# An attention block with a routed feed-forward: LayerNorm of transposed tokens along the partitions instead of transposing normalised tokens on TensorE

## What is computed

```python
x = x + xattn(layernorm(x), ctx)        # 16 heads of 64; ctx has 192 features
x = x + ffn(layernorm(x))               # 8 experts, the best 2 of each token

def layernorm(x): return (x - mean(x)) / sqrt(var(x) + 1e-5)      # over the 256 features
def xattn(x, ctx):
    q, k, v = x @ w_q, ctx @ w_k, ctx @ w_v                       # 256x1024, 192x1024
    return softmax(q k^T / 8) v @ w_o + b_o
def ffn(x):
    g = softmax(x @ gate); keep the 2 largest of 8, divide by their sum
    return sum over experts of g_e * (relu(x @ W1_e + b1_e) @ W2_e + b2_e)
```

## Time and profile before

| | |
|---|---|
| median of 3 runs | 1580.46 us (1580.43 to 1581.63) |
| the profiled execution | 1580.22 us |
| its span in the trace | 1578.5 us |
| PE busy | 1553.8 us, 98% |
| DVE, ACT, POOL busy | 75%, 70%, 52% |
| granted TensorE clock | 0.994 of full speed |

### The profile page before, as it was taken

One profiled execution on the slowest core, in us unless ns is written; L12 is line 12 of the kernel. 1 busy time (PEld: TensorE's weight loads), 2 busy tenths in 40 slices (PEclk: granted clock), 3 DMA queues, 4 the chain that ended last, 5 costly groups with the idle time before them and its releaser, 6 DMA issues.

```text
span 1578.5 us, 45424 instructions
## 1 busy us (share of the span) xinstructions
PE 1553.8 (98%) x14150; PEld 1454.0 (92%) x14151; DVE 1176.1 (75%) x3796; ACT 1108.0 (70%) x3357; POOL 818.1 (52%) x946
## 2 busy tenths in 40 slices
PE   8999999999999999999999999999999999999997
PEld 7899999999899999999999989998899999999997
DVE  4777777777777777777777777777788777777775
ACT  5677677677776777767767777676666676777774
POOL 2344545545554554554555455455456555555556
PEclk9999999999999999999999999999999999999999
DMA  6522111222111221211122211122799755555554
GB/s 201 145 72 74 60 60 60 77 90 72 62 60 60 67 94 66 74 60 60 63 75 89 74 60 60 60 67 81 241 231 249 144 86 85 89 86 90 84 84 61
DMA packets 105643, 145.05 MB, mean 92 GB/s; under 512 B 12736, under 2 KB 87616, under 8 KB 105344
## 3 DMA queue, kind: packets, MB, share of 16 engines
q1 hardware_dynamic: 60144, 89.00, 17.8%
q0 software_dynamic: 26816, 37.32, 13.7%
q10 hardware_dynamic: 18640, 18.19, 4.4%
HBM read 77.09 MB, written 67.38 MB: 92 GB/s over the span
## 4 chain that ended last, share of the span: by engine, by line
issue 47%; POOL 22%; PE 9%; DVE 7%; DMA 6%; DVEq 3%; ACT 2%; POOLq 2%; ACTq 1%; SPq 0%
POOL lists L662 7%; DMA out<-stage_room,number 6%; PE bank_a L1404 4%; POOL prob L669 3%; DVE hid L1332 3%; POOL rstd L648 2%; DVE stage_room L1349 2%; POOL stage_room L711 2%; POOL stage_room L707 2%; POOL out L735 2%; DVEq L1344 1%; PE bank_v L1437 1%; POOLq L729 1%; PE bank_s L1422 1%; DVEq L1323 1%
## 5 line engine op out<-in xcount | busy, mean ns | idle before, releaser
L669 POOL TENSOR_TENSOR prob<-prob,inv 128x512 f32<-128x512 f32 x256 | 271.4, 1060 | 520.3 <-DVE inv L956 519.6
L777 ACT ACTIVATE prob<-bank_s,low 128x128 f32<-128x128 f32 x1024 | 363.3, 376 | 40.9 <-DVE low L951 40.9
L735 POOL DMA_INDIRECT out<-stage_room,number x142 | 231.8, 1632 | 53.9 <-issue 53.1
L951 DVE TENSOR_REDUCE low<-bank_s 128x4 f32<-128x512 f32 x256 | 175.4, 685 | 98.0 <-PE bank_s L1422 97.9
L777 ACT ACTIVATION_READ_ACCUMULATOR prob<-bank_s,low 128x1 f32 x1024 | 221.1, 216 | 0.0
L770 ACT ACTIVATE probt<-bank_t 128x512 f32<-128x512 f32 x256 | 153.4, 599 | 89.6 <-PE bank_t L1411 89.6
L1050 DVE SCALAR_TENSOR_TENSOR stage_room<-xin,wo_t 128x256 f32<-128x256 f32 x480 | 178.8, 426 | 0.0
L807 ACT ACTIVATE ot_h<-bank_v 128x512 fp32r<-128x512 f32 x128 | 77.4, 604 | 138.4 <-PE bank_v L1437 138.4
L885 ACT ACTIVATE hidt_h<-hid 128x512 fp32r<-128x512 f32 x142 | 89.7, 632 | 117.4 <-DVE hid L1332 112.2
L1411 PE MATMUL bank_t<-ident,prob 128*128 128x128 f32 x1024 | 161.9, 281 | 4.0 <-POOL prob L669 4.0
L1404 PE MATMUL bank_a<-xt_l,wq_h 128*128 128x256 f32 x512 | 152.4, 298 | 0.3 <-DVE xt_l L966 0.3
(11 more groups left out here) (231 smaller groups left out, 4728.9 us busy)
## 6 DMA issues: line engine op xcount, KB each, us to landing
stage_room<-lists ACTq DMA_DIRECT2D x67, 265.0 KB
halves<-stage_room SPq DMA_DIRECT2D x32, 512.0 KB
homes<-halves SPq DMA_DIRECT2D x16, 1024.0 KB, 6.4
xin<-in_x SPq DMA_DIRECT2D x32, 256.0 KB, 2.8
stage_room<-in_x SPq DMA_DIRECT2D x32, 256.0 KB
stage_room<-in_w SPq DMA_DIRECT2D x32, 256.0 KB, 4.3
out<-stage_room SPq DMA_DIRECT2D x32, 256.0 KB, 2.2
cin<-in_ctx SPq DMA_DIRECT2D x32, 128.0 KB, 2.6
```

The costliest lines, as they stand in the source:

```text
L669: pool.tensor_tensor(prob[:, n % 4, :, :], prob[:, n % 4, :, :], wide(inv[:, n % 4, :], P), ALU.mult).then_inc(s_norm.sem, 1)
L735: pool.indirect_dma_start(out, bass.IndirectOffsetOnAxis(ap=number[:, u, b:b + 1], axis=0), ysum[:, u, b, :], None, compute_op=ALU.add).th ...
L777: e = act.activation(prob[:, n % 4, h, :], bank_s[n % 2][:, h * P:(h + 1) * P], ACT.Exp, bias=low[:, n % 4, h:h + 1], scale=-1.0, accum_ou ...
L951: dve.tensor_reduce(low[:, n % 4, :], bank_s[n % 2][:, :].rearrange("p (h k) -> p h k", h=4), AX.X, ALU.min).then_inc(s_low.sem, 1)
```

## The change

The host also passes `x_t`, the tokens transposed. SP loads the pair's 256 columns of it as `xraw` (feature per partition, between `xin` and `cin`). The statistics are still taken from `xin` by DVE and POOL, which now writes 1/sqrt over the variance in `mean_var`. SP (`ln_through`) waits for it, stores the 128x4 numbers to DRAM (`ln_rows`), waits for the store and loads them back as one row broadcast to all partitions (`ln_all`). DVE subtracts the mean and multiplies in place, two operations over 128x512 elements that read `ln_all` with a step of four words (`normalise_turned`, in slot 3 after the reciprocal). ACT writes the high part from `xraw` in slot 4, behind `copy_t` and ahead of `exps`; DVE writes the low part in slot 4 (`low_of_tokens`). Event `t0` with its four transposes is gone, and so are L1019's two operations into `xn`. The 15 remaining events get fixed banks (`BANK_OF`). The reciprocal of unit 3 moves from slot 4, behind `lowest`, to the end of slot 3. The three router scores of slot 3 are made in slots 1 and 2: 8, 6, 0 and 2. In pass -1 the broadcast is made by four matmuls instead of by DMA (`first_statistics`).

```diff
+    BANK_OF = {"q10": 0, "k10": 1, "o0": 2, "k11": 3, "q11": 0, "o1": 1, "v10": 2, "v11": 3,
+               "q00": 0, "k00": 1, "q01": 2, "k01": 3, "v00": 1, "f0": 0, "v01": 2}
-        [("o1", FROM0), ("t0", NEXT)],
+        [("o1", FROM0)],
...
+            def ln_through(sp, it):
+                if not isinstance(it, int) or it > 0:
+                    sp.wait_ge(ln_in, it * 16)
+                wait(sp, pool_step, it, "rstd1")
+                sp.dma_start(ln_rows, mean_var[:, 0, :, :]).then_inc(ln_out, 16)
+                sp.wait_ge(ln_out, it * 16 + 16)
+                wait(sp, xn_step, it - 1, "xn")
+                sp.dma_start(ln_all.rearrange("p t b k -> p (t b k)"), ln_rows.rearrange("t b k -> (t b k)").rearrange(
+                    "(o n) -> o n", o=1).to_broadcast([P, 4 * P])).then_inc(ln_in, 16)
...
                         load_x(it)
+                        ln_through(sp, it)
...
+                        if n == 4 and has(it, NEXT):
+                            wait(act, a_full, it, "q11")
+                            wait(act, xn_step, it, "xn")
+                            act.activation(xt[0][:, 0:DC, :], xraw.rearrange("p c b t -> p c (b t)"),
+                                           ACT.Copy).then_inc(xa_hi.sem, 1)
...
+                    dve.tensor_tensor(xraw[:, :, :, :], xraw[:, :, :, :], of_tokens(it, 0), ALU.subtract).then_inc(xn_step.sem, 1)
+                    wait(dve, xn_step, it, "centred")
+                    dve.tensor_tensor(xraw[:, :, :, :], xraw[:, :, :, :], of_tokens(it, 1), ALU.mult).then_inc(xn_step.sem, 1)
...
-                X_SCORES = {1: (0, 5), 2: (5, 6), 3: (11, 3), 5: (14, 2)}
+                X_SCORES = {1: [(0, 8)], 2: [(8, 3), (11, 3)], 5: [(14, 2)]}
...
-                    if kind == "t":
-                        wait(pe, ln1_step, it, "ln1")
-                        for b in range(2):
-                            for c in range(DC):
-                                last = pe.transpose(dst[:, (2 * c + b) * P:(2 * c + b + 1) * P],
-                                                    xn[:, b, c * P:(c + 1) * P], ident[:, :])
```

More of the change, by code:

```diff
@@ L359, in by_products, with a_bank @@
                 return isinstance(it, int) and it < 1
[L361 to L367, removed]
+            def a_bank(name):
+                return bank_a[BANK_OF[name]]
             def bank_before(it, name):
+                same = [n for n, _ in A_EVENTS if BANK_OF[n] == BANK_OF[name]]
                 if not isinstance(it, int):
[L372 to L376, removed]
+                    k = same.index(name) - 1
+                    return (it if k >= 0 else it - 1), same[k]
+                order = [(j, n) for j in range(-1, PAIRS + 1) for n in a_full.present(j) if n in same]
+                k = order.index((it, name)) - 1
                 return order[k] if k >= 0 else (it, None)
@@ L1035, in rows_of @@
                     dve.wait_ge(sent, (it - 1) * 64 + 16)
-                    normalise(it, 1, x1, [rows[:, b, 0:D] for b in range(2)])
+                    normalise(it, x1, [rows[:, b, 0:D] for b in range(2)])
                 def x_scores(it, first, many):
@@ L1140, in body @@
                         if n == 5 and has(it, NEXT) and not by_products(it):
-                            x_scores(it, *X_SCORES[n])
+                            for first, many in X_SCORES[n]:
+                                x_scores(it, first, many)
+                        if n == 4 and has(it, NEXT):
+                            low_of_tokens(it)
                         made_in = it - 1 if n == 0 else it
@@ L1184, in body @@
                             gate_max(it)
+                            after_step(it, "bn2_1")
+                        if n == 3 and has(it, NEAR[4][1]):
+                            inverse(it, NEAR[4][0], 3)
                         if n in X_SCORES and n < 5 and has(it, NEXT) and not by_products(it):
[L1186 removed]
+                            for first, many in X_SCORES[n]:
+                                x_scores(it, first, many)
                 steps_of_table = [0]
@@ L1567, in keep_busy, with first_statistics @@
                                   skip_group_check=True)
+                def first_statistics():
+                    wait(pe, pool_step, -1, "rstd1")
+                    pe.wait_ge(made, 20)
+                    for k in range(2):
+                        for b in range(2):
+                            last = pe.matmul(bank_s[1][:, (2 * k + b) * P:(2 * k + b + 1) * P],
+                                             mean_var[:, 0, b, k:k + 1].to_broadcast([P, P]), ident[:, :],
+                                             start=True, stop=True, skip_group_check=True)
+                    last.then_inc(ln_first, 1)
                 def gate_means():
```

118 lines of the change are left out of this document (68 added, 50 removed).

## The result

| | us, median (runs) | ratio to before, 95% interval |
|---|---|---|
| before | 1580.6 (6) | |
| changed | 1588.37 (1584.91 to 1589.22, 6 runs) | 1.0049 [1.0037, 1.0061] |

The changed kernel is slower by 0.5%, 7.8 us. That is above the 0.2% that can be told from nothing and outside the range of the forecast. The profiled execution took 1587.79 us with a span of 1586.0, 7.5 more than the span of before.

What follows compares the result with a forecast made beforehand. PE was taken as the bound, without gaps worth naming in the loop. 1580.22 us profiled + 0.7 start - 13.6 transposes + 13.3 chain gave 1580.6 us, no change, with a range of 1575 to 1586 us.

Steps and rivals of the forecast that it cites:

- The transposes, -0.44 us a pass.: PE between `o1` and `values`, slot 3: four transposes gone, 0.65 us becomes 0.21, at most 13.6 us in 31 passes.
- The chain of slot 4, +0.43 us.: From T, start of slot 4's PE transposes: ACT's copy delays DVE's low parts, `k00` loads 0.43 us late; 13.3 us.
- The early reciprocal: 0.: POOL scales unit 3 about 1.5 us earlier, clear of the tokens' low part; PE did not wait for that unit.
- may be lost here for nothing: DVE in slot 3: 1.7 us could be lost at no cost before the low part starts at T+1.85.
- the low part meets POOL's work and the chain grows by 0.1 to 0.2 us, 3 to 6 us: Rival, slot 4: slower by 3 to 6 us; 8% together with an overrun of slot 3.
- DVE in slots 1 to 3: 0.: Moved scores and two operations on `xraw` fit into freed waits and gaps: 0, at most 2 us in all.
- my bound of 1.46: Slot 3, DVE: longest time in us for each operation on `xraw`, where the 1.7 us are used up.
- my 0.61: Slot 3, DVE: lower time in us for each strided operation on `xraw`, what L1157 costs; 0.61 to 1.0 taken.
- The broadcast: 0.: Statistics through DRAM, slots 1 to 3: 6.0 us needed of 7.9 us, 1.9 us in hand.
- The start, +0.7.: Pass -1: 256 KB of `xraw` ahead of the weights PE waits for, +0.7 us, bounds 0 to 1.3.
- `k00` never waits: Extreme of the shorter-chain rival, slot 4: no wait, 1567.3 us; that rival had 20% for a gain over 3.2 us.

Runs made afterwards that it cites:

- b2: Kernel before, with three of the four transposes of the tokens left out in the looped passes: 1569.45 us, ratio 0.9932.
- d2: Changed kernel, unit 3's reciprocal right behind DVE's multiplication, POOL's last send behind unit 3's scaling, ACT's copy of `xraw` ahead of `copy_t`: 1567.64 us, ratio 0.9918.
- e1: Changed kernel, POOL's last send behind unit 3's scaling and ACT's copy of `xraw` ahead of `copy_t`; reciprocal left at the end of slot 3: 1567.14 us, ratio 0.9911.
- d1: Changed kernel, unit 3's reciprocal right behind DVE's multiplication and POOL's last send behind unit 3's scaling: 1582.95 us, ratio 1.0015.
- a2: Changed kernel, statistics stored apart in DRAM so each loads as 128 neighbouring elements, the store in 512 pieces of 4 bytes: 1773.55 us, ratio 1.1229.
- d4: Changed kernel, unit 3's reciprocal moved back to slot 4 behind `lowest`: 1589.00 us, ratio 1.0056.
- e2: Changed kernel, unit 3's reciprocal right behind DVE's multiplication and ACT's copy of `xraw` ahead of `copy_t`; sends not moved: 1589.34 us, ratio 1.0054.
- a1: Changed kernel, ACT's copy of `xraw` in slot 4 moved ahead of `copy_t`: 1587.98 us, ratio 1.0048.
- d3: Changed kernel, each statistic read from 512 neighbouring elements of `ln_all` instead of with a step (wrong values): 1584.94 us, ratio 1.0027.

## Why the prediction was wrong

- *The transposes, -0.44 us a pass.* Right. b2: 0.35 for three of four; the floor of d2 and e1: 0.44 for four.
- *The chain of slot 4, +0.43 us.* Its mechanism and its place are right to the instruction: `k00` waits for `xt_l`, in 29 passes, and the low part starts at T+1.85. With POOL out of the way (d1) the chain is as worked out within 0.01 us and the pass within 0.05. Those 0.05 are a small slip of mine: the low part was to end at T+4.93 and the load to go at T+4.98, but the load needs 0.11 us behind that end, in d1 as before. In the changed kernel the term is +0.63 (34.35 - 34.16 + 0.44), 0.15 more than in d1, and that is the collision.
- ***The step that failed: "The early reciprocal: 0. It would let POOL scale unit 3 by about 1.5 us earlier, out of the way of the low part of the tokens."*** I let POOL start when its operand was ready, and left out what POOL has to do first: two sends, which no step of mine followed. They ended at T+1.06, not T-0.74, because of my own slot 3: I wrote that POOL scales "to 722.7, multiply to 723.3" and that the rest "may be lost here for nothing", and looked only at DVE's slack. The wait that DVE hands to POOL (0.68 us in the scaling, 0.70 in the send) was the one that cost. The rival "the low part meets POOL's work and the chain grows by 0.1 to 0.2 us, 3 to 6 us" is what happened (0.15 us in the step, 0.17 in the chain, 5.1 us over the loop), and I had given it a part of 8%.
- *DVE in slots 1 to 3: 0.* For DVE right: no unit is late by it. The operations took 1.06 and 1.85 us; the second is above my bound of 1.46, but because POOL held it. From the start of the first to DVE's next instruction it is 2.87 us (724.92 to 727.79), where I had 2.2, with 1.7 more to lose. The Trainium skill's 1.73 ns a column (Vector Engine (DVE) Microarchitecture Reference, The SBUF access granule: adjacent pairs), measured there for one source that hops 4 KiB at every element, would be an estimated 0.96 us for the strided subtraction. Measured is 1.06 against 0.66, (1.06 - 0.66) / 512 = 0.78 ns a column more, where the page has 0.68 more. The trace agrees with the page within 0.1 us, and speaks against my 0.61.
- *The broadcast: 0.* Right, with 1.2 us in hand.
- *The start, +0.7.* The first `lowest` is at 24.80 us in place of 23.60, +1.2 and within the bounds; by the start of pass 1 it is +0.5, and the kernels of the table scatter by 4 us there (a2 aside).
- *One pass.* The sum had no term for pass 29: 4.5 us of the span's 7.5 in the profiled execution. Nothing in my steps looked at whether a wait that comes once and was hidden would stay so. How much of it is in the medians was not measured apart; the stall is in every kernel of the table, always at the last send of pass 29, 1.3 to 6.9 us long. Where that send stands ahead of the scaling of unit 3 it made the pass 0.7 to 5.1 us longer (a2 aside), where it stands behind, by nothing. The three longest (changed, d4 and e2: 3.7 to 5.1) are those where the granted clock fell to 0.50 afterwards; the others lost 0.7 to 2.2. This too is POOL's queue: the scaling that waits behind the sends is the one of the step that failed.

So the range was too narrow by one mechanism on an engine that I took to be idle, and by one pass in 32. By the profiled execution either alone would have stayed inside it: 1587.79 less 4.5 is 1583.3, less 5.1 is 1582.7. My rival "`k00` never waits" was worked out at 1567.3 us; e1, two moves away from the change, measures 1567.1. What stays open: what the stall of POOL's issue is, why the clock fell behind a wait of 2.98 us and not behind a1's 2.63, and the 0.07 us by which `copy_t` is late in d3.

## What to carry to other kernels

When work moves between engines, follow the queue of every engine that it makes wait, not only the one that it is put on: the instruction behind the one that is held, and the one behind that. An operation that used to read a PSUM bank and now reads SBUF twice is a different operation beside POOL, whatever its length alone. And if a fix of one late step gains nothing (a1), look at what ends last at the same place: two moves that were worth nothing alone or little (a1 0.0%, d1 0.3%) were worth 1.3% together.

## What the runs showed of the hardware

- Of a DVE operation with two SBUF operands and a POOL scaling that overlap, one is held until the other has ended: 1.77 us for a DVE operation of 0.66 (a1), 1.73 for a POOL operation of 1.05 (changed). A DVE operation with an operand in PSUM is not held (0.66 beside 1.04, before).
- POOL's issue of an indirect DMA is held too: 1.69 us in place of 0.99, ending 0.88 us behind DVE's multiplication, as if it had begun when that ended; in e1 the last send takes 1.27 us and ends 0.88 us behind the low part. The sends beside the router's scores, which read 256 columns from two places of SBUF, are not held (1.05 and 1.00 us, changed). The Trainium skill (SBUF — State Buffer, A bandwidth-pool intuition that's wrong) tells something near it of a DVE copy in a two-port mode, which keeps GpSimd from writing descriptors until about 0.115 us behind the copy's end. The same page (Who interferes with whom) has it that a `tensor_tensor` did not stall a DMA; here one with two SBUF inputs does go with the longer issue, and why it does and the scores do not is not shown.
- Small pieces: from the store of 2 KB to the load behind it 2.9 us with 128 pieces, 10.4 with 512.
- PE's granted clock was 0.50 for 6.8 us around the end of one wait of 2.98 us, and a step of its matmuls 0.21 us in place of 0.12 (pass 29, changed).
